# Second expert layer of a four-stage network: transposed shares and bias product moved into their own batch, top-two chain spread over the batch, bias product as one rounded pass over 24 divided rows

## What is computed

```python
scores = jnp.maximum((x @ gate_W + gate_b) / TEMP, EPS)      # EPS 1e-4, TEMP 1
p = jax.nn.softmax(scores, axis=-1)
_, topk_idx = jax.lax.top_k(p, K)                            # K = 2 of E = 8
w = jnp.maximum(p, W_THRES)                                  # 0.1
total = jnp.take_along_axis(w, topk_idx, axis=-1).sum(-1, keepdims=True)
comb = jnp.where(topk_mask, w / total, 0)
y = jnp.einsum('bsd,edf->bsef', x, expert_W) + expert_b
out = jnp.einsum('bsef,bse->bsf', y, comb) / K
x = x + out
```

## Time and profile before

| | us |
|---|---|
| median of 3 runs | 2227.72 (2227.47 to 2229.32) |
| the profiled execution's own time | 2226.19 |
| its span | 2224.4 |
| the last stage, from its first instruction to the end | 1951.8 to 2224.4 |
| one batch of that stage | 29.8 to 29.9 |
| busy over the span: TensorE matmuls | 1909.3 (86%) |
| VectorE | 1656.6 (74%) |
| GpSimd | 1427.7 (64%) |
| ScalarE | 1241.3 (56%) |

### The profile page before, as it was taken

How to read it: one execution, slowest core, us unless ns; L and a number is a source line. 1 busy time by engine, 2 the same in 40 slices (tenths; PEclk the granted TensorE clock), 3 DMA queues, 4 the chain that set the end, 5 groups by cost and what they waited for, 6 DMA issues and landing times. The chain is left out here.

```text
span 2224.4 us, 32244 instructions
## 1 busy us (share of the span) xinstructions
PE 1909.3 (86%) x9910; PEld 1116.9 (50%) x9910; DVE 1656.6 (74%) x2326; ACT 1241.3 (56%) x2642; POOL 1427.7 (64%) x1164
## 2 busy tenths in 40 slices
PE   2499999999973999975799999999999998759998
PEld 1244444444422899972345454545454433347776
DVE  4477788787744646530799999999999999836664
ACT  1066666676662433325787777777778675323332
POOL 7334444543334344430899999999999999834444
PEclk9599999999875999987999999999999999969999
DMA  3554545544234454430413131222213130021100
GB/s 80 108 103 96 110 107 116 113 99 122 69 123 149 84 88 76 75 51 19 162 42 130 58 114 75 97 91 81 106 66 121 42 132 30 0 78 39 38 26 22
DMA packets 231224, 185.68 MB, mean 83 GB/s; under 512 B 148729, under 2 KB 201601, under 8 KB 231058
## 3 DMA queue, kind: packets, MB, share of 16 engines
q1 hardware_dynamic: 216178, 162.61, 25.9%
q0 software_dynamic: 13296, 17.77, 4.6%
q10 hardware_dynamic: 1584, 3.24, 0.5%
HBM read 134.07 MB, written 49.49 MB: 83 GB/s over the span
## 5 line engine op out<-in xcount | busy, mean ns | idle before, releaser
L1817 POOL TENSOR_TENSOR mb_dbu<-mb_dtu,mb_bbc 128x1024 f32<-128x1024 f32 x256 | 598.6, 2360 | 5.2 <-DVE mb_da_ps L1974 2.4
L473 ACT ACTIVATE ex_plain<-at_t_ps 128x512 f32<-128x512 f32 x512 | 289.5, 595 | 178.9 <-PE at_t_ps L851 176.8
L1974 DVE TENSOR_TENSOR_SCAN mb_da_ps<-mb_da_ps,mb_dbu 128x1024 f32<-128x1024 f32 x160 | 365.3, 2283 | 4.0 <-ACT mb_da_ps L1867 3.3
L2009 PE MATMUL mb_y_ps<-mb_hc,lw_ident 128*128 128x512 f32 x640 | 311.7, 610 | 43.1 <-DVE mb_hc L1981 42.7
L610 DVE TENSOR_REDUCE at_mx<-at_s_ps 128x2 f32<-128x1024 f32 x256 | 310.9, 1219 | 47.7 <-PE at_s_ps L860 46.2
L860 PE MATMUL at_s_ps<-ex_w 48*128 48x512 f32 x512 | 226.4, 504 | 37.4 <-DVE at_mx L610 24.2
L851 PE MATMUL at_t_ps<-ex_w 64*128 64x512 f32 x512 | 220.0, 487 | 11.6 <-ACT ex_plain L473 6.4
L1823 POOL TENSOR_TENSOR mb_hp<-mb_hp,mb_cbc 128x1024 f32<-128x1024 f32 x96 | 226.1, 2356 | 0.0
L1201 POOL DMA_INDIRECT x<-m_o,m_xs x71 | 113.7, 1602 | 173.3 <-DMA x<-m_o,m_xs 106.6
L1972 DVE TENSOR_TENSOR_SCAN mb_hp<-mb_da_ps,mb_dbu 128x1024 f32<-128x1024 f32 x96 | 218.9, 2280 | 6.4 <-POOL mb_dbu L1817 5.4
L2009 PEld LDWEIGHTS mb_y_ps<-mb_hc,lw_ident 128*128 128x128 f32 x640 | 118.2, 192 | 201.8 <-issue 126.5
(11 more groups left out here) (322 smaller groups left out, 4117.8 us busy)
## 6 DMA issues: line engine op xcount, KB each, us to landing
mb_bbc<-mb_scr SPq DMA_DIRECT2D x64, 512.0 KB, 6.0
mb_cbc<-mb_scr SPq DMA_DIRECT2D x64, 512.0 KB, 5.7
ex_w<-at_scr SPq DMA_DIRECT2D x384, 64.0 KB, 2.3
m_xs<-rt_rows SPq DMA_DIRECT2D x71, 129.0 KB, 2.1
at_scr<-at_qk_hi SPq DMA_DIRECT2D x32, 256.0 KB
at_scr<-at_qk_lo SPq DMA_DIRECT2D x32, 256.0 KB
at_xin<-in_x SPq DMA_DIRECT2D x32, 128.0 KB, 2.3
ex_plain<-in_x SPq DMA_DIRECT2D x8, 512.0 KB
```

The lines of the kernel that those rows point to most:

```text
L473: act.activation(probs[:, c, h, :], t_ps[:, k % 2, :], ACT.Exp, scale=SCALE).then_inc(exp_done, 1)
L1817: pool.tensor_tensor(dbu[:, q % 3, :, :], dtu_2, bbc[:, 2 * p:2 * p + 2, :], ALU.mult).then_inc(S["dbu_ready"], 1)
L1974: dve.tensor_tensor_scan(da, da, add, 0.0, ALU.mult, ALU.add).then_inc(S["scan_done"], 1)
L2009: last = pe.matmul(y_ps[:, v % 2, :], ident[:, :], src[:, j, :], start=False, stop=(q == tile_last[v] and j == 1))
```

## The change

- The product of `comb` and the biases is done over 24 rows in one rounded pass: the rows of `combT` are high part, low part, high part of `comb`, and those of `eb_3` high, high, low part of `expert_b`. Four operations on VectorE make `eb_3` once, three per batch make `comb_3`. The input `eb` is handed over three times below each other, and one small input `m1_parts` is new.
- `turn_comb(n)` and `take_comb(n)` are in batch n itself, behind unit 3, into a PSUM tensor of their own (`c_ps`). `biases` follow units 5 and 12. `b_ps` has one buffer instead of two.
- The units of batch 0 no longer wait for `comb`.
- VectorE adds the bias product at the end of its tiles, behind units 6 and 14, and GpSimd's last add of a tile (`finish`) is done for two tiles at a time, behind units 7 and 15.
- The chain for batch n + 1 is placed anew: `variance` behind unit 0, `normalise` 2, `turn_rows` 5, `gate` 8, `scores` 8, `first_choice` 10, `second_choice` 12, `shares` 14, `low` 9, `root` 1, `take_rows` 5, `exponents` 9. Before, variance and root were made two batches ahead.
- In the prologue ScalarE divides all four weight blocks before `take_rows(0)`, and GpSimd no longer waits for `comb` between them.

The core of the diff:

```diff
-        eb = sb("eb", [E, D])
+        eb, eb_hi, parts_of = sb("eb", [3 * E, D]), sb("eb_hi", [3 * E, D], F32R), sb("parts_of", [3 * E, 2])
+        eb_3 = sb("eb_3", [3 * E, D], F32R)
...
-        combT = sb("combT", [E, 2, T])
+        comb_3 = sb("comb_3", [P, 4, 3, E], F32R)
+        combT = sb("combT", [3 * E, 2, T], F32R)
...
+        c_ps = ctx.enter_context(nc.psum_tensor("m1_c_ps", [P, T], F32))
...
+                def finish(n, k):
+
+                    pool.wait_ge(S["odd_added"], 4 * (PAIRS - 1) * n + (PAIRS - 1) * (k + 1))
+                    pool.wait_ge(S["b_added"], 2 * n + k // 2 + 1)
+                    pool.tensor_tensor(x[:, n % XB, k, :], x[:, n % XB, k, :], odd[:, k, :], ALU.add).then_inc(S["tile_done"], 1)
 
                 for n in range(NB):
-                    for u in range(UNITS):
-                        if u % 2:
-                            add_odd(n, u)
-                        if u == 7 and n + 1 < NB:
+                    for u in range(1, UNITS, 2):
+                        add_odd(n, u)
+                        if u in (7, 15):
+                            finish(n, u // PAIRS - 1)
+                            finish(n, u // PAIRS)
+                        if u == 9 and n + 1 < NB:
                             low(n + 1)
...
+                    dve.wait_ge(S["comb_ready"], n + 1)
+                    wait(dve, S["combT_ps"], n)
+                    top_steps(dve.tensor_copy(comb_3[:, :, 0, :], comb[:, n % 2, :, :]))
+                    dve.tensor_copy(comb_3[:, :, 2, :], comb_3[:, :, 0, :])
+                    dve.tensor_tensor(comb_3[:, :, 1, :], comb[:, n % 2, :, :], comb_3[:, :, 0, :], ALU.subtract).then_inc(S["comb_3_ready"], 1)
...
                     for u in range(0, UNITS, 2):
                         accumulate(n, u)
+                        if u in (6, 14):
+                            add_biases(n, u // PAIRS - 1)
                         if n + 1 < NB:
                             if u == 0:
+                                variance(n + 1)
+                            if u == 2:
                                 normalise(n + 1)
-                            if u == 6:
+                            if u == 8:
                                 scores(n + 1)
...
                 def turn_rows(n):
 
                     pe.wait_ge(S["xn_ready"], n + 1)
-                    wait(pe, S["combT_ready"], n)
+                    wait(pe, S["z_ready"], n)
...
                 turn_rows(0)
                 gate(0)
-                turn_comb(0)
                 for n in range(NB):
                     pe.wait_ge(S["xT_lo_ready"], n + 1)
-                    pe.wait_ge(S["combT_ready"], n + 1)
...
+                        if u == 3:
+                            turn_comb(n)
                         if n + 1 < NB:
-                            if u == 3:
+                            if u == 5:
                                 turn_rows(n + 1)
-                            if u == 6:
+                            if u == 8:
                                 gate(n + 1)
-                            if u == 14:
-                                turn_comb(n + 1)
+                        if u in (5, 12):
+                            biases(n, 0 if u == 5 else 2)
```

More of the change, by code:

```diff
@@ L1471, in _ @@
                 root(0)
-                upper(0)
-                upper(1)
+                for e in range(PAIRS):
+                    upper(e)
                 take_rows(0)
-                root(1)
                 exponents(0)
-                upper(2)
-                upper(3)
-                take_comb(0)
                 for n in range(NB):
-                    act.wait_ge(S["comb_ready"], n + 1)
                     for u in range(UNITS):
+                        if u == 1:
+                            act.wait_ge(S["comb_ready"], n + 1)
                         if u % 2:
                             weigh_odd(n, u)
+                        if u == 3:
+                            take_comb(n)
                         if n + 1 < NB:
-                            if u == 3:
+                            if u == 1:
+                                root(n + 1)
+                            if u == 5:
                                 take_rows(n + 1)
-                            if u == 7:
+                            if u == 9:
                                 exponents(n + 1)
-                            if u == 14:
-                                take_comb(n + 1)
-                        if u == 15 and n + 2 < NB:
-                            root(n + 2)
             @block.vector
@@ L1561, in accumulate @@
                     dve.wait_ge(S["o_ready"], UNITS * n + u + 1)
[L1562 to L1568, removed]
+                    wait(dve, S["acc_done"], q)
                     for a in range(2):
@@ L1623, in turn_comb @@
                 def turn_comb(n):
-                    pe.wait_ge(S["comb_ready"], n + 1)
+                    pe.wait_ge(S["comb_3_ready"], n + 1)
+                    wait(pe, S["combT_ready"], n)
                     for k in range(4):
-                        last = pe.transpose(f_ps[0:E, 0, k * P:(k + 1) * P], comb[:, n % 2, k, :], ident[:, :])
+                        last = pe.transpose(c_ps[0:3 * E, k * P:(k + 1) * P], comb_3[:, k, :, :].rearrange("p s e -> p (s e)").bitcast(F32), ident[:, :])
                     last.then_inc(S["combT_ps"], 1)
                 def biases(n, k):
-                    wait(pe, S["b_added"], 2 * n + k // 2 - 1)
+                    pe.wait_ge(S["combT_ready"], n + 1)
+                    wait(pe, S["b_added"], 2 * n + k // 2)
+                    pe.wait_ge(S["eb_ready"], 4)
                     for a in range(2):
-                        last = pe.matmul(b_ps[:, k // 2, a * D:(a + 1) * D], combT[:, n % 2, (k + a) * P:(k + a + 1) * P], eb[:, :], start=True, stop=True)
+                        last = pe.matmul(b_ps[:, a * D:(a + 1) * D], combT[:, n % 2, (k + a) * P:(k + a + 1) * P], eb_3[:, :], start=True, stop=True)
                     last.then_inc(S["b_ready"], 1)
@@ L1645, in _ @@
                         tok = slice(k * P, (k + 1) * P)
-                        if u % PAIRS == 0 and k % 2 == 0:
-                            biases(n, k)
                         if n == 0 and k == 0:
```

47 lines of the change are left out of this document (26 added, 21 removed).

## The result

| | us |
|---|---|
| before, median of 12 runs | 2227.47 (2222.15 to 2229.32) |
| changed, median of 12 runs | 2229.62 (2226.10 to 2233.01) |
| changed to before | 1.0017, 95% interval 1.0009 to 1.0024 |
| the profiled execution of the changed kernel, and its span | 2226.1, 2224.3 |
| busy: TensorE, VectorE, GpSimd, ScalarE | 1918.1, 1680.2, 1426.1, 1240.7 |

The change costs 0.17% (0.09% to 0.24%), inside the 0.2% that I called no change and at its edge. The stages ahead of the last one begin and end some 6 us apart between executions.

What follows compares the result with a forecast made beforehand. TensorE was taken as the bound before, VectorE's chain as the next. Prologue -9.0, batch 0 +1.8, batches -3.3, tail +0.85 and clock falls +11.9 gave +2.2 us: 2228.4 profiled, 2230 us median, range 2209 to 2238.

Steps and rivals of the forecast that it cites:

- batch at full clock: Last stage, one batch: VectorE's circle with GpSimd's stops closes in 29.3 us.
- six batches without falls: Last stage: each of six batches gets 0.55 us shorter, -3.3 us in all.
- start and tail together: Last stage's ends: earlier units -9.0 us, waits in batch 0 +1.8, last batch's finish as two operations +0.85.
- falls: Last stage: TensorE's clock drops behind the wait seven times, 1.7 us each, +11.9 us.
- (a): Bias product on TensorE: 0.45 us instead of 1.26, twice a batch, saving 1.6 us; bounds 0.24 and 1.26.
- (b): TensorE's wait for `comb` goes, since it is needed only after unit 3 of the next batch; 1.5 us per batch before.
- TensorE's own work: TensorE in one batch, without waits: 26.0 us from units, rows' transposes, gate, `comb` transposes and two bias products.
- (c): Prologue: units begin at 1974.1 instead of 1983.07, -9.0 us; waits of 0.8, 0.55 and 3.4 us give back +1.8.
- VectorE's circle: VectorE's chain, unit 10 to next rows: 24.8 us circle without stops, 4.1 us of GpSimd stops; TensorE waits 3.0 us.
- The clock: TensorE, last stage: waits of 3.0 us let the clock fall to 1.2 GHz, granted clock below 1 in each batch.
- rival of dearer falls: TensorE, last stage: each fall costs 3.4 us, twice as much; +14 us, 2242 us; chance 0.15.
- the first rival: TensorE, last stage: the clock holds through the 3 us gaps; -9.7 us, 2218 us; chance 0.17.

Runs made afterwards that it cites:

- e1_fill: Changed kernel plus ten unused 512-column matmuls ahead of the wait for `xn` in each batch but the last; 2221.4 us, 0.9974 of before.
- e2_variance: Changed kernel with variance(n + 2) behind unit 6 instead of variance(n + 1) behind unit 0; 2206.34 us, 0.9907 of before.
- e3_start: Changed kernel, but the first unit waits for `comb_3` of batch 0, undoing the prologue's gain alone; 2235.03 us, 1.0036 of before.
- e9_bias_fill5: Changed kernel with the old 8-row full-precision bias product at the new places, without `comb_3`, plus five filling matmuls; 2221.95 us, 0.9965 of before.
- e5_few_columns: Changed kernel with GpSimd's adds and finishes cut to 8 columns from batch 1, `low` to 8 from batch 2; 2206.79 us, 0.9911 of before.
- second profile: The changed kernel run and profiled once more, unaltered; 2233.55 us, 1.0030 of before, stage time 263.3 us.
- e4_low_out: Changed kernel with GpSimd's `low` alone cut to 8 of 512 columns from batch 2 on; 2231.84 us, 1.0026 of before.
- e8_warm: e2_variance plus 46 transposes of the identity ahead of the stage's first rows' transposes; 2205.06 us, 0.9902 of before.
- e11_late_finish: e2_variance with the second half of each batch's bias add and finishes moved into the next batch; 2200.15 us, 0.9878 of before.

## Why the prediction was right, and where it was not

The forecast was 2230 us and no measurable change; measured were 2229.62 and 1.0017. The mechanism, a circle through VectorE's chain that leaves TensorE one wait a batch, and a clock that falls behind it, is shown by e1_fill and e2_variance. Its terms, against the stage times of the first profile (258.3 and 258.35):

| term | forecast | measured |
|---|---|---|
| batch at full clock | 29.3 | 29.5 |
| six batches without falls | -3.3 | 6 x 29.5 - 179.5 = -2.5 |
| start and tail together | -9.0 + 1.8 + 0.85 = -6.35 | 72.3 - 78.8 = -6.5 |
| falls | 7 x 1.7 = +11.9 | 186.1 - 177.0 = +9.1 |
| sum | +2.2 | +0.1 |

Start and tail are the times outside the six batches: 23.2 and 49.1 us after, 25.4 and 53.4 before.

How close the number came is in part luck. The forecast for a profiled execution was 2228.4 us; the two profiled ones took 2226.1 and 2229.08, with stage times 0.1 and 5.0 us above the kernel before. And the row of start and tail agrees although its parts do not: the start by itself is worth 3.9 us (e3_start) and not 7.2, and the cheaper bias product gives 2.6 us behind the last `turn_rows` (e9_bias_fill5), where the forecast had a loss of 0.85. The two add up to the 6.5 us measured; no run undoes them together.

- **(a) Bias product.** 0.45 was close to 0.53, inside its bounds of 0.24 and 1.26. The estimate of 0.28 from the Trainium skill ("FP8 and Floating Point Precision", TensorE Precision Notes) was too low: by pace, 0.42 against 1.06 is two and a half times, not four. What I had not seen is that VectorE takes the gain back inside the circle (e9_bias_fill5).
- **(b) The wait for `comb`** went, as forecast.
- **TensorE's own work** was put at 26.0 us and is 26.7 (e5_few_columns). A pace of 0.233 instead of 0.228 makes 0.45 of the difference over 96 matmuls. It did not matter here, since VectorE set the batch.
- **(c) Prologue.** The first unit starts at 1973.35, forecast 1974.1. The waits of batch 0 were put at 0.8, 0.55 and 3.4; they are 1.75, 0.30 and 1.28 in the first profile and 0.50, 0.31 and 3.37 in the second. VectorE's part is the same in both: `w_lo`, of which GpSimd makes two blocks in one go (4.69 and 4.68 us), stops the scores, so that L1525 takes 2.09 and 2.08 us, which I had not foreseen, having walked GpSimd's new order for a batch and not for the prologue. What differs is the clock. At the start the low level ends 10.5 us behind the first transposes in the first profile and 13.3 in the second, so the units ahead of the first wait end sooner in the first, and the wait is longer. Then a fall in batch 0 of the first profile (from 1983.28 to 1986.69) took 1.5 us that were waited in the second; the other 0.55 us between the last waits (3.37 and 1.28) are `normalise`, whose passes take 1.93 us in the second and 1.38 in the first. The forecast of -7.2 for all of this was too large: of the 9 us by which the units begin earlier, 3.9 reach the end (e3_start), half of it clock.
- **VectorE's circle.** Stops of 4.1 us were forecast, 3.9 to 4.0 at the short operations and 0.4 to 0.5 in the passes of `normalise` were measured, at the operations named (`first_choice`'s multiplication, the end of the batch, `normalise`). The wait of 3.0 us came out as 2.53, since TensorE's own work is 0.7 us longer.
- **The clock.** This is the term that was mis-sized: seven falls of 1.7 us were forecast, one fall or none came behind each wait, for 1.5 or 3.0 us, four of six in the profiled execution. That the granted clock would be below 1 in each batch was wrong. The rival of dearer falls was half right: the double length exists, and waits of 2.5 us do not always bring a fall. The term came near (9.1 for 11.9) because fewer falls and dearer ones offset each other in part: four of 2.3 us on average for seven of 1.7. In the second profile the six batches lie 11.9 us above 177, for five falls, one of them behind the wait of 3.37 us, and a sixth fall lies behind them.
- The limit that the Trainium skill gives for an idle gap ("TensorE: Matmul & The Clock Gate", HAM oscillation) was not reached by any of these waits, and by that rule all six batches would have been 29.5 us and the time that of the first rival. The traces do not agree: 18 falls behind 24 waits of 2.4 to 2.6 us, 2 behind 7 of 1.4.

What decides whether a wait lets the clock fall stays open. Its length matters (18 of 24, 2 of 7, and none in e2_variance, whose six waits are 0.5 us), but the kernel before bore seven waits of 1.3 to 1.7 us for `comb`. The place alone does not decide it either: in batch 0 of five profiles (the changed kernel's first, e1_fill, e4_low_out, e8_warm, e11_late_finish) TensorE waited 1.6 to 1.9 us ahead of the transposes of `comb` and 0.30 us more behind them, and the clock fell each time. That second, short wait is one difference from the kernel before; no run takes it away alone.

## What to carry over

Close the circle before you judge a placement: add up every step from one unit to the same unit of the next batch, stops by other engines included, and move what needs no input from the circle (here the variance, 2.1 us a batch; then the bias add and the finishes) into the place where that engine waits anyway. Where TensorE must wait, a microsecond or two is not the whole price: here a wait of 2.5 us cost another 1.5 us a batch by the clock. Filling it gave 8.3 us in a stage of 258, and taking 2.1 us out of every circle, which also left only 0.5 us of wait, gave 23.6. Time saved counts only where it lies in the circle, and so does time paid: the rounded product gave TensorE 0.64 us there and cost VectorE as much, and the second product of a batch, outside the circle, was worth nothing while TensorE waited.

## What the runs showed that was not expected

- Stops can move instead of going away. With `low` gone (2.4 us of GpSimd in every batch), VectorE was stopped for 3.93 us instead of 3.89, by other operations. A chain in one line that runs beside adds bound to TensorE's units catches the next add instead. Only with the adds short too did they go (e5_few_columns).
- Which operations of VectorE stop: besides those with two SBUF operands (L1540) also those with one, a multiplication by a constant and a rounding copy (L1556 0.65, L1559 0.66 instead of 0.18); reductions never did. The Trainium skill ("GPSIMD Engine Reference", the row on SBUF interfaces) names both kinds, two SBUF inputs and a 2-port mode, and the trace agrees in the first; that those two run in such a mode no run here shows.
- The same program gives stage times 5 us apart by which waits meet a fall, so one profile of such a kernel is a draw. Ten matmuls of no use steadied it: six batches within 0.14 us.
